# Rewriting the last stage of a recurrent mixture-of-experts layer: other engines, another number of buffers, other order of transfers

## The chip, the cores and the metric

The kernel runs on one core of one Trainium2 chip. The metric is the device time of one execution in microseconds. Five engines matter: TensorE (PE in the profile, its weight loads PEld), VectorE (DVE), ScalarE (ACT), GpSimd (POOL) and SyncE (SP), which here only issues transfers. All of them work on SBUF, the on-chip memory of 128 partitions; DMA engines move data between it and HBM.

## The reference

The input x has 2 x 2048 tokens of 512 channels in float32. Cut to what matters:

```python
xn = layernorm(x)                          # (x - mean) / sqrt(var + 1e-5), each token
# a recurrent layer over the tokens of each sequence
x_conv = silu(conv4(xn) + conv_b)
delta, B_in, C_in = projections(x_conv)
h_t = exp(delta * A) * h_(t-1) + delta * B_in * x_conv     # 16 states per channel
s = sum_n(h * C_in) + xn * D_param
# a mixture of 8 experts, the best 2 of each token, capacity 1024
y = sum_over_2_choices(gate * (gelu(disp @ fc1_w + fc1_b) @ fc2_w + fc2_b))
g = silu(y)
out = x + s * g
```

## The kernel before

Three functions run one after the other, each in a block of its own with its own semaphores and memory; all engines meet between two of them. `front` computes mean and rstd of every token, the routing, and the inputs of the recurrence. `main_loop` runs the experts on TensorE beside the recurrence on VectorE; it leaves `sum_n(h * C_in)` in HBM as `s_rows` and the experts' weighted sum y as `moe_rows`. `tail` is the last stage and the only function that differs between the two kernels: `out = x + (xn * D + s) * silu(y)`.

`tail` goes over the 4096 tokens in NP = 16 pieces of 256 tokens. A piece is a tile of 128 partitions x 2 x 512 values, 512 KB. Each piece has three loads (x into `t_x`, `s_rows` into `t_s`, `moe_rows` into `t_y`) and one store (`t_o`). There are RING = 4 buffers of each kind. For a piece p with its buffer u = p mod 4 the steps are:

- `normalise` (L1177, VectorE): two instructions of 128x512, `o = (x - mean) * rstd`. It waits for all three loads (`in{u}`) and for the store that last used the buffer (`out{u}`).
- `skip` (L1162, GpSimd): `o = o * D`, one instruction of 128x1024, when `xn` says that normalise is done.
- `silu` (L1152, ScalarE): `g = silu(y)`, into a buffer of its own.
- `combine` (L1182, L1185, L1187, VectorE): `o = o + s`, `o = o * g`, `o = o + x`, each one instruction of 128x1024, each waiting for the one before through a semaphore. The first also waits for `skip`.

VectorE runs normalise of piece p+1 ahead of combine of piece p. The order of the transfers is that of SyncE's program: the loads of the first four pieces, and then, for each piece, its store (L1133, when `sum` says that the piece is done) and the three loads (L1126 to L1128) of the piece four later. Each engine's program is a loop of four rounds of four pieces (VectorE's last round is written out).

Of the kernel before, what the change touches and what calls it, by code (L numbers as in the profile page):

```python
# [29 lines left out]
ALU = mybir.AluOpType  # L30
ACT = mybir.ActivationFunctionType
AX = mybir.AxisListType.X
ds = bass.ds

P = 128
B, T, D = 2, 2048, 512
# [11 lines left out]
NT = S // P  # L48
# [30 lines left out]
def memory(nc, ctx):  # L79
    def sb(name, shape, dt=F32):  # L80
        return ctx.enter_context(nc.sbuf_tensor(name, shape, dt))

    def psum(name, shape):
        return ctx.enter_context(nc.psum_tensor(name, shape, F32))

    def sems(prefix, names):
        return {n: ctx.enter_context(nc.semaphore(prefix + n)) for n in names.split()}

    return sb, psum, sems
# [1005 lines left out]
def tail(nc, a, dr, keep, out):  # L1095

    with ExitStack() as ctx:
        sb, psum, sems = memory(nc, ctx)
        TPP = 2
        RING = 4  # L1100
        PC, NP = TPP * P, NT // TPP
        d_row = sb("t_D", [P, D])
        s = sb("t_s", [P, RING, TPP, D])
        y, x = sb("t_y", [P, RING, TPP, D]), sb("t_x", [P, RING, TPP, D])
        g, o = sb("t_g", [P, RING, TPP, D]), sb("t_o", [P, RING, TPP, D])
        rings = " ".join(f"in{u} out{u}" for u in range(RING))
        s_ = sems("t_", f"consts {rings} silu xn skip whole gated sum")
        block = ctx.enter_context(nc.Block())

        def over_rings(eng, body):  # L1110

            with eng.Fori(0, NP // RING) as i:
                for u in range(RING):
                    body(RING * i + u, i, u)

        @block.sync
        def _(sp):
            for u in range(RING):
                sp.sem_inc(s_[f"out{u}"], 16)  # L1119
            sp.dma_start(d_row[:], a["D"].to_broadcast([P, D])).then_inc(s_["consts"], 16)  # L1120

            def load(c, half, p, u):


                sp.wait_ge(s_["sum"], p + 1)
                sp.dma_start(x[:, u], a["x"][ds(c, 1), :, TPP * half:TPP * (half + 1), :].rearrange("o p j d -> p (o j) d")).then_inc(s_[f"in{u}"], 16)  # L1126
                sp.dma_start(s[:, u], dr.s[ds(p * PC, PC)].rearrange("(j p) d -> p j d", p=P)).then_inc(s_[f"in{u}"], 16)  # L1127
                sp.dma_start(y[:, u], dr.y[ds(p * PC, PC)].rearrange("(j p) d -> p j d", p=P)).then_inc(s_[f"in{u}"], 16)  # L1128

            def store(p, u):  # L1130

                sp.wait_ge(s_["sum"], p + RING + 1)
                sp.dma_start(out[ds(p, 1)].rearrange("o (j p) d -> p (o j) d", p=P), o[:, u]).then_inc(s_[f"out{u}"], 16)  # L1133

            for u in range(RING):
                load(u // 2, u % 2, u, u)
            with sp.Fori(1, NP // RING) as i:
                for u in range(RING):
                    store(RING * i + u - RING, u)
                    load(RING // 2 * i + u // 2, u % 2, RING * i + u, u)  # L1140
            for u in range(RING):
                store(NP - RING + u, u)
            for u in range(RING):
                sp.wait_ge(s_[f"out{u}"], 16 * NP // RING + 16)

        @block.scalar
        def _(act):
            def silu(p, i, u):
                act.wait_ge(s_[f"in{u}"], 48 * i + 48)

                act.wait_ge(s_["gated"], p + 1)
                act.activation(g[:, u], y[:, u], ACT.Silu).then_inc(s_["silu"], 1)  # L1152

            over_rings(act, silu)

        @block.gpsimd
        def _(pool):
            pool.wait_ge(s_["consts"], 16)

            def skip(p, i, u):  # L1160
                pool.wait_ge(s_["xn"], p + 1)
                pool.tensor_tensor(o[:, u], o[:, u], d_row[:].unsqueeze(1).to_broadcast([P, TPP, D]), ALU.mult).then_inc(s_["skip"], 1)  # L1162

            over_rings(pool, skip)

        @block.vector
        def _(dve):
            for name in ("whole", "gated", "sum"):
                dve.sem_inc(s_[name], RING)

            def normalise(p, i, u):
                dve.wait_ge(s_[f"in{u}"], 48 * i + 48)

                dve.wait_ge(s_[f"out{u}"], 16 * i + 16)  # L1174
                for j in range(TPP):
                    mean, rstd = (keep[k][:].rearrange("p c j -> p (c j)")[:, ds(TPP * p + j, 1)] for k in ("mean", "rstd"))
                    op = dve.tensor_scalar(o[:, u, j, :], x[:, u, j, :], mean, rstd, ALU.subtract, ALU.mult)  # L1177
                op.then_inc(s_["xn"], 1)

            def combine(p, u):  # L1180
                dve.wait_ge(s_["skip"], p + 1)
                dve.tensor_tensor(o[:, u], o[:, u], s[:, u], ALU.add).then_inc(s_["whole"], 1)  # L1182
                dve.wait_ge(s_["whole"], p + RING + 1)  # L1183
                dve.wait_ge(s_["silu"], p + 1)  # L1184
                dve.tensor_tensor(o[:, u], o[:, u], g[:, u], ALU.mult).then_inc(s_["gated"], 1)  # L1185
                dve.wait_ge(s_["gated"], p + RING + 1)
                dve.tensor_tensor(o[:, u], o[:, u], x[:, u], ALU.add).then_inc(s_["sum"], 1)  # L1187


            normalise(0, 0, 0)  # L1190
            with dve.Fori(0, NP // RING - 1) as i:  # L1191
                for u in range(RING):
                    normalise(RING * i + u + 1, i + (u + 1) // RING, (u + 1) % RING)
                    combine(RING * i + u, u)
            for u in range(RING):
                if u < RING - 1:
                    normalise(NP - RING + u + 1, NP // RING - 1, u + 1)
                combine(NP - RING + u, u)


def build(nc, a, out):
    dr = Scratch(nc)
    with ExitStack() as ctx:
        sb, _, _ = memory(nc, ctx)
        keep = {
            "mean": sb("mean_keep", [P, NCH, TPC]),
            "rstd": sb("rstd_keep", [P, NCH, TPC]),
            "b1": sb("b1_keep", [P, E * HID // P]),
            "neg_a": sb("neg_a_keep", [P, N, KT]),
            "row": sb("row_keep", [P, E + 1, TILES], I32),  # L1210
            "add_row": sb("add_row_keep", [P, E + 1, TILES], I32),
            "gate": sb("gate_keep", [P, E, TILES]),
            "ct": sb("ct_keep", [P, NT, N]),
            "going": sb("going_keep", [P, NCH + 1]),
        }
        front(nc, a, dr, keep)
        main_loop(nc, a, dr, keep)
        tail(nc, a, dr, keep, out)
# [63 lines left out]
```

## Time and profile before

| what | value |
|---|---|
| median of 3 runs | 2216.96 us (2212.52 to 2220.56) |
| the profiled execution, time | 2222.13 us |
| the profiled execution, span from first to last instruction | 2220.3 us |
| last stage in it: first load issued / end of the span | 2101.4 us / 2220.3 us |

Times in the rows are microseconds from the start of the span. "Busy" is time in which an engine worked on an instruction. The share of the whole span (VectorE 88%, TensorE 85%) is an average over all three stages; the last stage is the stretch from 2101 us on, in which TensorE does nothing.

### The profile page before, as it was taken

To read this page: it belongs to the slowest core of one execution; us is meant where nothing else is said; L and a number is where in the kernel's file an instruction comes from. 1 tells how busy PE (TensorE), PEld (TensorE's weight loads), DVE (VectorE), ACT (ScalarE), POOL (GpSimd) and SP (SyncE) were. 2 spreads that over 40 slices of the span, in tenths; PEclk is the share of its full clock that TensorE was granted. 3 is DMA by queue.
4 is the path that set the end of the run, shared out by engine and by line. 5 is a ranking of instruction groups with operands and counts; after the bars stand their busy time and mean duration, and the time that the engine had idled before them with its cause. 6 is when DMAs were issued, how large, how long until landed. Compare 5 with 4: busy or idle time off the path is not lost. (4 is left out here: it accounts for less than half of the span.)

```text
span 2220.3 us, 30939 instructions
## 1 busy us (share of the span) xinstructions
PE 1890.7 (85%) x9160; PEld 1483.9 (67%) x9160; DVE 1955.3 (88%) x2102; ACT 1177.1 (53%) x1714; POOL 1383.9 (62%) x606
## 2 busy tenths in 40 slices
PE   6666729999999999999999999999999999999500
PEld 3222327788788778877887788777877787788400
DVE  6788848989998999899989998998899889998699
ACT  3365635466556555565555556555655565556121
POOL 1267657566756775667566756675667566756454
PEclk9787959999999999999999999999999999999855
DMA  9624354123512441244124412441244124312597
GB/s 292 226 59 93 82 206 95 57 67 128 114 62 67 129 110 62 67 141 102 57 67 144 100 57 71 139 100 57 71 150 89 57 71 144 95 57 81 117 319 250
DMA packets 89192, 246.96 MB, mean 111 GB/s; under 512 B 13296, under 2 KB 14320, under 8 KB 77808
## 3 DMA queue, kind: packets, MB, share of 16 engines
q1 hardware_dynamic: 70640, 207.30, 28.1%
q0 software_dynamic: 18176, 37.83, 9.3%
q8 instruction: 72, 1.18, 0.2%
q10 hardware_dynamic: 256, 0.26, 0.1%
q14 instruction: 48, 0.39, 0.1%
HBM read 173.66 MB, written 71.70 MB: 111 GB/s over the span
## 5 line engine op out<-in xcount | busy, mean ns | idle before, releaser
L976 POOL TENSOR_TENSOR ub_sb<-u_sb,brow_sb 128x1024 f32<-128x1024 f32 x256 | 642.6, 2510 | 463.0 <-DVE a_sb L1071 460.2
L1071 DVE TENSOR_TENSOR_SCAN a_sb<-a_sb,state,ub_sb 128x512 f32<-128x512 f32 x512 | 876.6, 1752 | 12.1 <-issue 7.8
L738 PE MATMUL pm<-xTh,w1l 128*128 128x512 f32 x1024 | 429.4, 419 | 14.9 <-DVE part L1059 6.5
L738 PE MATMUL pm<-w2h,hl 128*128 128x512 f32 x1024 | 423.9, 414 | 0.0
L740 PE MATMUL pm<-xTh,w1h 128*128 128x512 f32 x1024 | 405.9, 396 | 0.0
L739 PE MATMUL pm<-xTl,w1h 128*128 128x512 f32 x1024 | 403.5, 394 | 0.0
L740 PE MATMUL pm<-w2h,hh 128*128 128x512 f32 x1024 | 402.7, 393 | 0.0
L739 PE MATMUL pm<-w2l,hh 128*128 128x512 f32 x1024 | 399.6, 390 | 0.0
L1037 DVE SCALAR_TENSOR_TENSOR s_acc<-pt,ct_keep,s_acc 128x512 f32<-128x512 f32 x480 | 353.1, 736 | 28.3 <-PE pt L768 27.4
L768 PE MATMUL pt<-m_ident,a_sb 128*128 128x128 f32 x2048 | 311.2, 275 | 54.0 <-DVE a_sb L1071 46.3
L768 PEld LDWEIGHTS pt<-m_ident,a_sb 128*128 128x128 f32 x2048 | 251.7, 140 | 131.1 <-issue 55.6
L879 ACT ACTIVATE a_sb<-delta_sb,neg_a_keep 128x512 f32<-128x512 f32 x512 | 330.1, 713 | 6.5
L902 ACT ACTIVATE hh<-pm,b_keep 128x512 fp32r<-128x512 f32 x256 | 176.3, 689 | 219.0 <-PE pm L740 214.9
L1046 DVE TENSOR_TENSOR hl<-pm,hh 128x512 fp32r<-128x512 f32 x256 | 174.6, 682 | 70.7 <-ACT pm L903 66.0
L738 PEld LDWEIGHTS pm<-xTh,w1l 128*128 128x128 f32 x1024 | 196.4, 192 | 50.2 <-DVE part L1059 8.6
L740 PEld LDWEIGHTS pm<-xTh,w1h 128*128 128x128 f32 x1024 | 195.3, 191 | 45.1
L740 PEld LDWEIGHTS pm<-w2h,hh 128*128 128x128 f32 x1024 | 192.6, 188 | 43.5
L872 ACT ACTIVATE state<-a_sb,going_keep 128x4 f32 (+1 forms) x96 | 28.6, 298 | 362.3 <-PE pt L768 362.3
L739 PEld LDWEIGHTS pm<-xTl,w1h 128*128 128x128 f32 x1024 | 196.8, 192 | 33.5
L739 PEld LDWEIGHTS pm<-w2l,hh 128*128 128x128 f32 x1024 | 194.0, 189 | 32.8
L1059 DVE SCALAR_TENSOR_TENSOR part<-pm,gate_keep,part 128x512 f32<-128x512 f32 x256 | 188.5, 736 | 30.7 <-PE pm L740 28.3
L738 PEld LDWEIGHTS pm<-w2h,hl 128*128 128x128 f32 x1024 | 193.4, 189 | 30.9
(130 smaller groups left out, 2286.0 us busy)
## 6 DMA issues: line engine op xcount, KB each, us to landing
w_raw<-in_w SPq DMA_DIRECT2D x64, 1024.0 KB, 5.0
brow_sb<-b_chunks SPq DMA_DIRECT2D x128, 256.0 KB, 3.7
moe_rows<-zeros_sb SPq DMA_DIRECT2D x5, 2048.0 KB, 17.2
xin_sb<-in_x SPq DMA_DIRECT2D x8, 1024.0 KB, 6.2
xn_rows<-xn_sb SPq DMA_DIRECT2D x8, 1024.0 KB, 8.5
delta_chunks<-ln_sb SPq DMA_DIRECT2D x8, 1024.0 KB
u_chunks<-u_now_sb SPq DMA_DIRECT2D x16, 512.0 KB
delta_sb<-delta_chunks SPq DMA_DIRECT2D x8, 1024.0 KB, 8.6
```

The costliest lines, as they stand in the source:

```text
L738: pe.matmul(out, sl, mh, start=start, stop=False)
L739: pe.matmul(out, sh, ml, start=False, stop=False)
L740: return pe.matmul(out, sh, mh, start=False, stop=stop)
L768: mm = pe.transpose(pt[:, bank(s, last), kt * P:(kt + 1) * P], abuf[:, m, kt, tb * P:(tb + 1) * P], ident[:])
L872: act.activation(state[:, ds(q * NPQ * KT + (m - NPQ) * KT, KT)].unsqueeze(2), ends, ACT.Copy, scale=going(e + 1)).then_inc(s_["carried"], 1)
L879: op = act.activation(abuf[:, m, kt, :], delta[:, kt, :], ACT.Exp, scale=keep["neg_a"][:].rearrange("p n k -> p (n k)")[:, ds(col, 1)])
L902: act.activation(hh[:, g, j, :], pm[:, j, :], ACT.Gelu, bias=bias)
L976: pool.tensor_tensor(ub[:, h], u[:, 2 * h:2 * h + 2, :], brow[:, m % 2:m % 2 + 1, :].to_broadcast([P, 2, CH]), ALU.mult).then_inc(s_["bmul ...
L1037: dve.scalar_tensor_tensor(out=acc, in0=h, scalar=c, in1=acc, op0=ALU.mult, op1=ALU.add).then_inc(s_["summed"], 1)
L1046: dve.tensor_tensor(hl[:, g, j, :], pm[:, j, :], hh[:, g, j, :].bitcast(F32), ALU.subtract).then_inc(s_["h_free"], 1)
L1059: dve.scalar_tensor_tensor(out=part[:, t, :], in0=pm[:, t % 4, :], scalar=gate, in1=part[:, t, :], op0=ALU.mult, op1=ALU.add).then_inc(s_[ ...
L1071: op = dve.tensor_tensor_scan(abuf[:, m, 2 * h + k, :], abuf[:, m, 2 * h + k, :], ub[:, h, k, :], state[:, ds(col, 1)], ALU.mult, ALU.add)
```

## The change

`tail` is written anew. ScalarE normalises: two `activation` instructions of 128x512 per piece with the function Identity, `o = rstd * x + shift`, where `shift = -mean * rstd` is computed once for all tokens by one VectorE instruction. ScalarE also takes silu, now in place in `t_y`. VectorE does four instructions of 128x1024 per piece: `* D`, `+ s`, `* silu(y)`, `+ x`. GpSimd has no instruction left in the stage. There are 12 buffers instead of 4 and no `t_g`, the code is unrolled, and the loads of 12 pieces are issued before the first store. Each piece has its own semaphores, one for x and s together, one for y, one for the store.

```diff
-        RING = 4
+        RING = 12
...
-            for u in range(RING):
-                load(u // 2, u % 2, u, u)
-            with sp.Fori(1, NP // RING) as i:
-                for u in range(RING):
-                    store(RING * i + u - RING, u)
-                    load(RING // 2 * i + u // 2, u % 2, RING * i + u, u)
+            for p in range(RING):
+                load(p)
+            for p in range(NP):
+                store(p)
+                if p + RING < NP:
+                    load(p + RING)
...
-            def skip(p, i, u):
-                pool.wait_ge(s_["xn"], p + 1)
-                pool.tensor_tensor(o[:, u], o[:, u], d_row[:].unsqueeze(1).to_broadcast([P, TPP, D]), ALU.mult).then_inc(s_["skip"], 1)
...
+            act.wait_ge(s_["shift"], 1)
+
+            def normalise(p):
+                u = p % RING
+                act.wait_ge(s_[f"xs{p}"], 32)
+                if p >= RING:
+                    act.wait_ge(s_[f"out{p - RING}"], 16)
+                for j in range(TPP):
+                    t = TPP * p + j
+                    op = act.activation(o[:, u, j, :], x[:, u, j, :], ACT.Identity, bias=shift[:, t:t + 1],
+                                        scale=keep["rstd"][:].rearrange("p c j -> p (c j)")[:, t:t + 1])
+                op.then_inc(s_["xn"], 1)
+
+            def silu(p):
+                u = p % RING
+                act.wait_ge(s_[f"y{p}"], 16)
+                act.activation(y[:, u], y[:, u], ACT.Silu).then_inc(s_["silu"], 1)
+
+            for p in range(NP):
+                normalise(p)
+                silu(p)
...
+            dve.scalar_tensor_tensor(out=shift[:], in0=mean, scalar=-1.0, in1=rstd, op0=ALU.mult, op1=ALU.mult).then_inc(s_["shift"], 1)
+            dve.wait_ge(s_["consts"], 16)
+            for p in range(NP):
+                u = p % RING
+                dve.wait_ge(s_["xn"], p + 1)
+                dve.tensor_tensor(o[:, u], o[:, u], d_row[:].unsqueeze(1).to_broadcast([P, TPP, D]), ALU.mult).then_inc(s_["skip"], 1)
                 dve.wait_ge(s_["skip"], p + 1)
                 dve.tensor_tensor(o[:, u], o[:, u], s[:, u], ALU.add).then_inc(s_["whole"], 1)
...
-                dve.tensor_tensor(o[:, u], o[:, u], g[:, u], ALU.mult).then_inc(s_["gated"], 1)
...
+                dve.tensor_tensor(o[:, u], o[:, u], y[:, u], ALU.mult).then_inc(s_["gated"], 1)
```

On VectorE this is what stands in its program for one piece before, in the middle of the loop (normalise of the next piece, then combine of this one; ISA and REGISTER_ALU rows are waits and addresses):

```order
L1177 ISA [waits t_out2,t_in2]
L1177 TENSOR_SCALAR t_o<-t_x,mean_keep,rstd_keep 128x512
L1177 ISA
L1177 TENSOR_SCALAR t_o<-t_x,mean_keep,rstd_keep 128x512
L1182 TENSOR_TENSOR t_o<-t_o,t_s 128x1024 [waits t_skip]
L1183 REGISTER_ALU
L1185 TENSOR_TENSOR t_o<-t_o,t_g 128x1024 [waits t_silu,t_whole]
L1187 TENSOR_TENSOR t_o<-t_o,t_x 128x1024 [waits t_gated]
```

and this at the start of VectorE's part of the stage now; the last four rows come sixteen times:

```order
L1159 SCALAR_TENSOR_TENSOR t_shift<-mean_keep,rstd_keep 128x32
L1164 TENSOR_TENSOR t_o<-t_o,t_D 128x1024 [waits t_xn,t_consts]
L1166 TENSOR_TENSOR t_o<-t_o,t_s 128x1024 [waits t_skip]
L1169 TENSOR_TENSOR t_o<-t_o,t_y 128x1024 [waits t_silu,t_whole]
L1171 TENSOR_TENSOR t_o<-t_o,t_x 128x1024 [waits t_gated]
```

The two normalising instructions and all waits for transfers have left VectorE; a multiply by `t_D` has come, and no wait for GpSimd is left.

On ScalarE the beginning of the stage is now this, the first piece and the normalising of the second (`t_xs0` and `t_y0` are the landings of the first piece's x and s, and of its y):

```order
L1143 ACTIVATE t_o<-t_x,t_shift,rstd_keep 128x512 [waits t_xs0,t_shift]
L1143 ACTIVATE t_o<-t_x,t_shift,rstd_keep 128x512
L1150 ACT_TABLE_LOAD
L1150 ACTIVATE t_y<-t_y 128x1024 [waits t_y0]
L1143 ACTIVATE t_o<-t_x,t_shift,rstd_keep 128x512 [waits t_xs1]
```

One ACT_TABLE_LOAD stands in the whole stage, where the loop before had one in each of its four rounds.

On SyncE, the queue of the transfers, this follows the 36 loads of the first twelve pieces; four such groups of a store and three loads come, and then the last stores without a load between them:

```order
L1121 DMA out<-t_o 128x2x512 [waits t_sum]
L1115 DMA t_x<-in_x 128x1024
L1116 DMA t_s<-s_rows 128x2x512
L1117 DMA t_y<-moe_rows 128x2x512
L1121 DMA out<-t_o 128x2x512 [waits t_sum] x12
```

Before, twelve loads stood ahead of the first store, and twelve such groups followed.

## Rows read from the trace of the kernel before

**Rows 1.** Chain that ended last, from 2085 us on, by line:

```profile
by line: DVE t_o L1185 36.9%; DVE t_o L1182 13.5%; issue 11.1%; DVE t_o L1177 10.7%; DMA t_y<-moe_rows 7.0%; DVE t_o L1187 1.4%; DVEq L1177 1.4%; SPq L1126 0.8%; SPq L1127 0.7%; DVEq L1183 0.4%; SPq L1128 0.3%; SPq L1120 0.3%; DVEq L1174 0.
```

**Rows 2.** Timeline of one round: start, duration, engine, line, operation [idle before]:

```profile
2147.11 1.00 DVE L1177 TENSOR_SCALAR t_o<-t_x,mean_keep,rstd_keep 128x512 f32<-128x512 f32 x2
...
2148.02 1.22 DVE L1182 TENSOR_TENSOR t_o<-t_o,t_s 128x1024 f32<-128x1024 f32 x1
2148.18 3.26 POOL L1162 TENSOR_TENSOR t_o<-t_o,t_D 128x1024 f32<-128x1024 f32 x1 [3.34 <-DVE t_o L1177]
...
2149.27 3.25 DVE L1185 TENSOR_TENSOR t_o<-t_o,t_g 128x1024 f32<-128x1024 f32 x1
...
2152.55 1.22 DVE L1187 TENSOR_TENSOR t_o<-t_o,t_x 128x1024 f32<-128x1024 f32 x1
2153.70 1.00 DVE L1177 TENSOR_SCALAR t_o<-t_x,mean_keep,rstd_keep 128x512 f32<-128x512 f32 x2
```

**Rows 3.** The last piece on VectorE, same columns:

```profile
2213.02 1.22 DVE L1182 TENSOR_TENSOR t_o<-t_o,t_s 128x1024 f32<-128x1024 f32 x1
2214.27 1.23 DVE L1185 TENSOR_TENSOR t_o<-t_o,t_g 128x1024 f32<-128x1024 f32 x1
2215.53 1.23 DVE L1187 TENSOR_TENSOR t_o<-t_o,t_x 128x1024 f32<-128x1024 f32 x1
```

**Rows 4.** The first pieces on ScalarE, VectorE and GpSimd, same columns:

```profile
2109.23 1.00 DVE L1177 TENSOR_SCALAR t_o<-t_x,mean_keep,rstd_keep 128x512 f32<-128x512 f32 x2 [20.56 <-DMA t_y<-moe_rows]
2109.30 1.28 ACT L1152 ACT_TABLE_LOAD   x1 [23.98 <-DMA t_y<-moe_rows]
2110.32 2.34 POOL L1162 TENSOR_TENSOR t_o<-t_o,t_D 128x1024 f32<-128x1024 f32 x1 [21.03 <-DVE t_o L1177]
...
2113.93 1.06 ACT L1152 ACTIVATE t_g<-t_y 128x1024 f32<-128x1024 f32 x1 [2.27 <-DMA t_y<-moe_rows]
...
2117.76 1.06 ACT L1152 ACTIVATE t_g<-t_y 128x1024 f32<-128x1024 f32 x1 [2.77 <-DMA t_y<-moe_rows]
...
2121.51 1.06 ACT L1152 ACTIVATE t_g<-t_y 128x1024 f32<-128x1024 f32 x1 [2.70 <-DMA t_y<-moe_rows]
```

**Rows 5.** Windows: length, busy us (count) of each engine, clock, DMA share, GB/s:

```profile
core 0: us, PE busy (x) PEld busy (x) DVE busy (x) ACT busy (x) POOL busy (x), PEclk, DMA share, GB/s
2112.00:2120.00 8.00, 0.00 (x0) 0.00 (x0) 5.79 (x5) 2.11 (x2) 3.92 (x2) 0.50 1.01 399
2134.00:2199.95 65.95, 0.00 (x0) 0.00 (x0) 65.27 (x51) 13.13 (x12) 32.57 (x10) 0.50 0.96 320
2214.00:2216.00 2.00, 0.00 (x0) 0.00 (x0) 1.93 (x3) 0.00 (x0) 0.00 (x0) 0.50 0.68 262
```

**Rows 6.** DMA issues of the stage: all packets, and s of the first piece:

```profile
DMA packets 15506, 33.84 MB, mean 282 GB/s; under 512 B 1040, under 2 KB 1040, under 8 KB 15504
...
L1127 SPq DMA_DIRECT2D t_s<-s_rows x1: 427/427/427, 2101.9 to 2101.9; - x1
DMA to landing us min/median/max: 6.0/6.0/6.0
```

**Rows 7.** ScalarE's groups by form over the whole span: count, busy us, mean ns:

```profile
L879 ACT ACTIVATE a_sb<-delta_sb,neg_a_keep 128x512 f32<-128x512 f32 x512 | 330.1, 713 | 6.5
...
L377 ACT ACTIVATE z_sb<-pT,chan_sb 128x512 f32<-128x512 f32 x32 | 20.1, 679 | 33.9 <-DVE back_sb L587 33.7
...
L354 ACT ACTIVATE xnT_sb<-conv_sb 128x512 f32 x28 | 15.6, 616 | 8.8 <-DVE conv_sb L506 8.8
```

**Rows 8.** Transfers that SyncE's queue issued, start, duration of the issue:

```profile
2106.47 0.47 SPq L1126 DMA_DIRECT2D t_x<-in_x  x1
2106.99 1.98 SPq L1127 DMA_DIRECT2D t_s<-s_rows  x1
2109.02 1.96 SPq L1128 DMA_DIRECT2D t_y<-moe_rows  x1
```

More of the change, by code:

```diff
@@ L1099, in tail @@
         TPP = 2
-        RING = 4
+        RING = 12
         PC, NP = TPP * P, NT // TPP
[L1102 to L1107, printed above, removed]
+        d_row, shift = sb("t_D", [P, D]), sb("t_shift", [P, NT])
@@ L1108, in tail @@
+        s, y, x, o = (sb(f"t_{n}", [P, RING, TPP, D]) for n in "syxo")
+        parts = " ".join(f"xs{p} y{p} out{p}" for p in range(NP))
+        s_ = sems("t_", f"consts {parts} shift silu xn skip whole gated sum")
         block = ctx.enter_context(nc.Block())
-        def over_rings(eng, body):
-            with eng.Fori(0, NP // RING) as i:
-                for u in range(RING):
-                    body(RING * i + u, i, u)
         @block.sync
         def _(sp):
-            for u in range(RING):
-                sp.sem_inc(s_[f"out{u}"], 16)
@@ L1120, in _ @@
             sp.dma_start(d_row[:], a["D"].to_broadcast([P, D])).then_inc(s_["consts"], 16)
-            def load(c, half, p, u):
-                sp.wait_ge(s_["sum"], p + 1)
-                sp.dma_start(x[:, u], a["x"][ds(c, 1), :, TPP * half:TPP * (half + 1), :].rearrange("o p j d -> p (o j) d")).then_inc(s_[f"in{u}"], 16)
-                sp.dma_start(s[:, u], dr.s[ds(p * PC, PC)].rearrange("(j p) d -> p j d", p=P)).then_inc(s_[f"in{u}"], 16)
-                sp.dma_start(y[:, u], dr.y[ds(p * PC, PC)].rearrange("(j p) d -> p j d", p=P)).then_inc(s_[f"in{u}"], 16)
@@ L1130, in store @@
[L1130 to L1135, printed above, removed]
-                load(u // 2, u % 2, u, u)
-            with sp.Fori(1, NP // RING) as i:
-                for u in range(RING):
-                    store(RING * i + u - RING, u)
-                    load(RING // 2 * i + u // 2, u % 2, RING * i + u, u)
-            for u in range(RING):
-                store(NP - RING + u, u)
@@ L1143, in _, with load @@
-            for u in range(RING):
-                sp.wait_ge(s_[f"out{u}"], 16 * NP // RING + 16)
+            def load(p):
+                u, c, half = p % RING, p // 2, p % 2
+                rows = slice(p * PC, (p + 1) * PC)
+                sp.dma_start(x[:, u], a["x"][c, :, TPP * half:TPP * (half + 1), :]).then_inc(s_[f"xs{p}"], 16)
+                sp.dma_start(s[:, u], dr.s[rows].rearrange("(j p) d -> p j d", p=P)).then_inc(s_[f"xs{p}"], 16)
+                sp.dma_start(y[:, u], dr.y[rows].rearrange("(j p) d -> p j d", p=P)).then_inc(s_[f"y{p}"], 16)
@@ L1146, in _, with store @@
+            def store(p):
+                sp.wait_ge(s_["sum"], p + 1)
+                sp.dma_start(out[p].rearrange("(j p) d -> p j d", p=P), o[:, p % RING]).then_inc(s_[f"out{p}"], 16)
+            for p in range(RING):
[5 more added lines that the diff above has]
+            for p in range(NP):
+                sp.wait_ge(s_[f"out{p}"], 16)
         @block.scalar
         def _(act):
[L1148 to L1158, printed above, removed]
-            def skip(p, i, u):
-                pool.wait_ge(s_["xn"], p + 1)
-                pool.tensor_tensor(o[:, u], o[:, u], d_row[:].unsqueeze(1).to_broadcast([P, TPP, D]), ALU.mult).then_inc(s_["skip"], 1)
-            over_rings(pool, skip)
+            act.wait_ge(s_["shift"], 1)
[9 more added lines that the diff above has]
+                op.then_inc(s_["xn"], 1)
@@ L1166, in _ @@
+            def silu(p):
[5 more added lines that the diff above has]
+                silu(p)
         @block.vector
         def _(dve):
[L1168 to L1178, printed above, removed]
@@ L1180, in combine @@
-            def combine(p, u):
+            mean, rstd = (keep[k][:].rearrange("p c j -> p (c j)") for k in ("mean", "rstd"))
+            dve.scalar_tensor_tensor(out=shift[:], in0=mean, scalar=-1.0, in1=rstd, op0=ALU.mult, op1=ALU.mult).then_inc(s_["shift"], 1)
+            dve.wait_ge(s_["consts"], 16)
+            for p in range(NP):
+                u = p % RING
+                dve.wait_ge(s_["xn"], p + 1)
+                dve.tensor_tensor(o[:, u], o[:, u], d_row[:].unsqueeze(1).to_broadcast([P, TPP, D]), ALU.mult).then_inc(s_["skip"], 1)
@@ L1181, in combine @@
                 dve.wait_ge(s_["skip"], p + 1)
                 dve.tensor_tensor(o[:, u], o[:, u], s[:, u], ALU.add).then_inc(s_["whole"], 1)
-                dve.wait_ge(s_["whole"], p + RING + 1)
+                dve.wait_ge(s_["whole"], p + 1)
                 dve.wait_ge(s_["silu"], p + 1)
-                dve.tensor_tensor(o[:, u], o[:, u], g[:, u], ALU.mult).then_inc(s_["gated"], 1)
-                dve.wait_ge(s_["gated"], p + RING + 1)
+                dve.tensor_tensor(o[:, u], o[:, u], y[:, u], ALU.mult).then_inc(s_["gated"], 1)
@@ L1187, in combine @@
+                dve.wait_ge(s_["gated"], p + 1)
                 dve.tensor_tensor(o[:, u], o[:, u], x[:, u], ALU.add).then_inc(s_["sum"], 1)
[L1190 to L1198, printed above, removed]
```

## The prediction, made before the changed kernel ran

> **What bounds the kernel now.** The change is in the last stage alone, so I first asked the chain of waits what that stage hangs on. From 2085 us on, its largest item is one VectorE instruction, the multiply of L1185, with 36.9% [rows 1]; nothing of a transfer stands there but 7.0%, the opening. Then I read the timeline of one piece in the middle [rows 2]. A piece takes 2153.70 - 2147.11 = 6.59 us, and VectorE is never idle in it: normalise 1.00, add 1.22, multiply 3.25, add 1.22, less small overlaps. What stands out is that the multiply takes 3.25 us where the adds of the same shape take 1.22. In the last piece the same L1185 takes 1.23 [rows 3]. The difference is GpSimd: in the middle its multiply runs from 2148.18 to 2151.44, and L1185 ends at 2152.52, 1.08 us after it. In the last piece GpSimd is idle. GpSimd suffers too: 3.26 us in company of the add, 2.34 alone [rows 2, 4]. So the two behave as if they took turns: GpSimd first waits about 1 us for the add, then VectorE waits until GpSimd is through. VectorE bounds the stage, and about 2 of its 6.6 us per piece are waiting.
>
> The Trainium skill's page "SBUF — State Buffer", section "SBUF: two separate sides", says just that: an exclusive lock on a port pair between a GpSimd instruction and a VectorE instruction with two SBUF inputs, in which the loser waits for the whole instruction. By that rule the 2 us go when GpSimd has no work. A view without it, in which L1185 is a slow multiply on its own account, is the last rival below; the 1.23 us of the last piece speak against it.
>
> Last, the transfers. In the steady stretch the DMA engines are busy to 0.96 at 320 GB/s; in the opening, when nothing but loads is queued, they give 399 GB/s at a share of 1.01 [rows 5]. 320 GB/s is simply VectorE's pace (a piece moves 4 x 0.524 = 2.10 MB; 2.10 MB / 6.59 us = 318 GB/s), yet the share of 0.96 says that there is little air left. That is the danger of this change.
>
> **The change, part by part.**
>
> *VectorE.* Per piece it drops two normalising instructions (1.00) and about 2.03 us of waiting, and takes on one multiply by D. I have no row of that multiply on VectorE. Bounds: below, the 1.22 us of an add of the same shape and operands; above, 3.25, what the other multiply takes now. I take 1.23, since L1185 without GpSimd took that [rows 3]. Each instruction waits for the one before through a semaphore: the starts in the last piece are 2213.02, 2214.27, 2215.53, so 1.255 us from one to the next. A piece is 4 x 1.255 = 5.02 us, sixteen are 80.3 us.
>
> *ScalarE.* Per piece it gets two instructions of 128x512 with scale and bias. The nearest rows are 616, 679 (a bias from SBUF) and 713 ns (a scale from SBUF) [rows 7]: between 1.23 and 1.43, I take 1.4. With silu's 1.06 that makes about 2.5 us a piece, half of VectorE's 5.02: covered, from the second piece on. If the cover were gone it would cost at most 2.5 us once per piece; it would take a table load of 1.28 twice per piece, and the program shows one in all.
>
> *The start.* Before, everything waited for y of the first piece, which was there at 2109.2 [rows 4]. Now x and s are enough for normalise; s was issued at 2101.9 and landed 6.0 later, at 2107.9 [rows 6]. Normalise to 2107.9 + 0.1 + 1.4 = 2109.4, and VectorE starts there. Silu of the first piece: table load at 2109.4, silu from 2110.7 to 2111.8; VectorE wants it after two instructions, at 2111.9, so it is just hidden. The one small VectorE instruction for `shift` runs during the loads' landing and costs nothing; if the landing did not cover it, it would be well under 1.2 us, once.
>
> *The end.* VectorE ends at 2109.4 + 80.3 = 2189.7. From the end of the last add now (2215.53 + 1.23 = 2216.76) to the end of the span (2220.3) there are 3.5 us for the last store. 2189.7 + 3.5 = 2193.2.
>
> *Do the transfers keep up?* Silu's waits show y of pieces 1, 2 and 3 landing before 2113.93, 2117.76 and 2121.51 [rows 4]: 3.8 us for the three loads of a piece, against VectorE's 5.02. From 2121.5, eight more pieces: the loads of twelve pieces are in at 2121.5 + 8 x 3.8 = 2151.9. SyncE does not run far ahead of that: after some ten transfers each issue takes 2 us where it took 0.5 [rows 8], so the first store, though its piece is done at 2114.4, goes out only near 2140 (ten transfers, some 12 us, before 2151.9) and lands about 2155. Who waits for it? ScalarE's normalise of piece 12, which VectorE wants at 2109.4 + 12 x 5.02 = 2169.6: 13 us to spare. Behind it come four groups of a store and three loads. At 399 GB/s a group takes 5.3 us, at the mixed rate of the middle 320 / 0.96 = 333 GB/s it takes 6.3: y of piece 15 is in between 2173 and 2177, ScalarE is done with it 2.5 us later, and VectorE wants it at 2184.7. Meanwhile finished pieces pile up: eleven stores (4 to 14) at 262 / 0.68 = 385 GB/s [rows 5] or 1.36 us each make 15 us, so the queue is empty between 2188 and 2192, when the last store arrives at 2189.7. That adds between 0 and 3 us; I take 0.
>
> *Unrolled code, more semaphores, more buffers.* Nothing but waits on landed transfers; I cost them at nothing because each engine's program now runs ahead of a transfer or of VectorE. If the first instructions came late, it would be paid once, 1 to 2 us.
>
> *Sum* against the profiled execution's own span: 2220.3 - 2193.2 = 27.1 us less, so 2222.13 becomes 2195. The profiled execution lies 5.2 us above the median of 2216.96; on the median the forecast is 2190 (-1.2%). By pieces: 16 x (6.59 - 5.02) = 25.1, and some 2 from the earlier start.
>
> **The rivals.**
>
> *A. The transfers become the bound.* The share of 0.96 speaks for it, the 399 GB/s of the opening against it. If the whole stage only gets 333 GB/s, 33.84 MB [rows 6] take 101.6 us from about 2102.5; the end is at 2204 + 1, 15 us less than now: 2202. The Trainium skill would put it between: "DMA: Bandwidth & Descriptors", section "Where 436 GB/s comes from", lets HBM bind at about 358 GB/s per core. An estimate from this page is 94.5 us of transfers and a time near 2194. The trace does not agree with 358 as a limit here, since it held 399 over 8 us; its chance is part of A's.
>
> *B. The gain is eaten elsewhere and nothing is to be measured.* Loads slower than the opening make ScalarE wait for the first store, which lies behind 36 loads. With 6.2 us for the loads of a piece, twelve take 74 and four groups of 6.2 + 1.4 another 30; with the last piece's work (2.5 + 5.0) and the store (3.5) that is 2102.5 + 115 = 2218. It needs loads at 254 GB/s, and none of the windows with loads alone shows that. Time 2214.
>
> *C. Slower.* L1185's 3.25 us are not GpSimd's doing but belong to a multiply beside transfers, and the new multiply by D takes as long. Then a piece is 2 x 1.255 + 2 x 3.27 = 9.05 us, the stage 144.8, the end 2257.7: time 2254. It decides against the change as soon as the four instructions average (2216.8 - 2109.4) / 64 = 1.68 us. For it: fifteen of sixteen L1185 are long. Against it: the last is not, and each long one ends 1.1 us after GpSimd.
>
> **How the numbers follow.** Runs of one kernel here lie within 0.2% of their median (2212.52 to 2220.56), so 0.3%, 6.7 us, is about what can be told from no change. The forecast has 0.83, A 0.10, B 0.04, C 0.03. The forecast's own range: DMA backlog 0 to +3, start 0 to +2, VectorE at 1.22 instead of 1.255 -2, the spread of the runs ±4: 2184 to 2199. For 8 in 10 over all cases I stretch it to A: 2183 to 2202. Faster by over 0.3% are the forecast and A and no others, 0.93; same 0.04; slower 0.03.
>
> **What would show it.** In the profile of the changed kernel: L1164, L1166, L1169 and L1171 all between 1.20 and 1.25 us and back to back, 5.0 us a piece (wrong if any is over 1.5: C); VectorE's first multiply near 2109.4; ScalarE busy half the time and waiting for VectorE nowhere; the idle time of VectorE between pieces, if any, ended by ScalarE, and ScalarE's by a transfer (A) or by `out0` (B); the first store issued near 2140; the last landing 2.7 to 6 us after its issue. The prediction is wrong if VectorE is idle for more than a few us after the second piece.

## The result, and the profile after

| | before | after |
|---|---|---|
| median of 6 runs | 2215.31 us (2211.73 to 2223.63) | 2185.38 us (2179.89 to 2192.14) |
| profiled execution, span | 2220.3 us | 2186.5 us |
| ratio of times, 95% interval | | 0.9856 [0.9833, 0.9879] |

The change takes 29.9 us, 1.35%, off the median; the ratio on record is not the quotient of the two medians, 0.9865, which lies inside its interval. The forecast was 2190 us. The last stage, from the issue of the load of D to the end of the span, was 119.3 us in the profiled execution before (2101.04 to 2220.3) and is 90.65 us now (2095.85 to 2186.5). That is 28.6 us; the rest of the 33.8 us between the two spans lies ahead of the stage, in code that is the same (experiment 9 shows that it comes and goes from run to run).

The groups of instructions of the last stage in the changed kernel (line, engine, operation, count, busy us, mean ns, idle time before and what ended it):

```profile
L1143 ACT ACTIVATE t_o<-t_x,t_shift,rstd_keep 128x512 f32<-128x512 f32 x32 | 24.3, 806 | 48.5 <-DMA t_s<-s_rows 48.5
L1171 DVE TENSOR_TENSOR t_o<-t_o,t_x 128x1024 f32<-128x1024 f32 x16 | 19.6, 1225 | 0.5
L1169 DVE TENSOR_TENSOR t_o<-t_o,t_y 128x1024 f32<-128x1024 f32 x16 | 19.6, 1225 | 0.6
L1166 DVE TENSOR_TENSOR t_o<-t_o,t_s 128x1024 f32<-128x1024 f32 x16 | 19.6, 1225 | 0.5
L1164 DVE TENSOR_TENSOR t_o<-t_o,t_D 128x1024 f32<-128x1024 f32 x16 | 19.5, 1218 | 8.3 <-ACT t_o L1143 8.3
L1150 ACT ACTIVATE t_y<-t_y 128x1024 f32<-128x1024 f32 x16 | 16.7, 1042 | 0.0
```

All four VectorE instructions take 1.22 us, the multiply by silu(y) too, and the multiply by D that no row of before had priced takes the same. VectorE waited once: 8.3 us before its first multiply. One piece in the middle, and the opening and the end, from the timeline (start, duration, engine, line):

```profile
2095.85 0.35 SPq L1110 DMA_DIRECT2D t_D<-in_D  x1
...
2102.72 1.52 ACT L1143 ACTIVATE t_o<-t_x,t_shift,rstd_keep 128x512 f32<-128x512 f32 x2 [22.09 <-DMA t_s<-s_rows]
...
2104.34 1.23 DVE L1164 TENSOR_TENSOR t_o<-t_o,t_D 128x1024 f32<-128x1024 f32 x1 [8.25 <-ACT t_o L1143]
...
2123.09 1.52 ACT L1143 ACTIVATE t_o<-t_x,t_shift,rstd_keep 128x512 f32<-128x512 f32 x2 [1.52 <-DMA t_s<-s_rows]
...
2124.00 1.22 DVE L1164 TENSOR_TENSOR t_o<-t_o,t_D 128x1024 f32<-128x1024 f32 x1
...
2125.25 1.22 DVE L1166 TENSOR_TENSOR t_o<-t_o,t_s 128x1024 f32<-128x1024 f32 x1
...
2126.51 1.23 DVE L1169 TENSOR_TENSOR t_o<-t_o,t_y 128x1024 f32<-128x1024 f32 x1
...
2127.77 1.23 DVE L1171 TENSOR_TENSOR t_o<-t_o,t_x 128x1024 f32<-128x1024 f32 x1
...
2128.91 1.22 DVE L1164 TENSOR_TENSOR t_o<-t_o,t_D 128x1024 f32<-128x1024 f32 x1
...
2137.37 1.72 SPq L1121 DMA_DIRECT2D out<-t_o  x1
...
2147.02 1.52 ACT L1143 ACTIVATE t_o<-t_x,t_shift,rstd_keep 128x512 f32<-128x512 f32 x2 [1.51 <-DMA t_s<-s_rows]
...
2152.15 1.52 ACT L1143 ACTIVATE t_o<-t_x,t_shift,rstd_keep 128x512 f32<-128x512 f32 x2 [2.66 <-DMA t_s<-s_rows]
...
2181.82 1.23 DVE L1171 TENSOR_TENSOR t_o<-t_o,t_x 128x1024 f32<-128x1024 f32 x1
```

A piece is 2128.91 - 2124.00 = 4.91 us where it was 6.59 [rows 2]. Within a piece the starts are 1.25 us apart; from the last instruction of a piece to the first of the next it is only 1.14. ScalarE's two normalising instructions wait for the landing of s each time, never for the store: the first store, issued at 2137.37, landed 12.2 us later, at 2149.6, and the inputs of piece 12, which takes its buffer, only at 2152.1. The windows over the loads alone and over nearly the full stage (length, busy of PE, PEld, DVE, ACT, POOL, clock, DMA share, GB/s), which answers to [rows 5]:

```profile
2108.00:2136.00 28.00, 0.00 (x0) 0.00 (x0) 27.42 (x24) 17.34 (x22) 0.00 (x0) 0.50 1.04 395
```

```profile
2108.00:2180.00 72.00, 0.00 (x0) 0.00 (x0) 70.49 (x60) 36.12 (x44) 0.00 (x0) 0.50 1.05 400
```

VectorE is busy 98%, and the transfers run at 400 GB/s over a window with loads alone up to 2137 and stores from there on, where they ran at 320 before.

### The profile page after: what moved, and what is told of

Same layout as the page of the kernel before. It is cut to its first block and busy times, and to the rows that moved or that the text cites. A ratio compares the mean times of both kernels' runs of the same rounds, so it can differ in the third digit from the quotient of the medians.

```text
span 2186.5 us, 30720 instructions
## 1 busy us (share of the span) xinstructions
PE 1892.6 (87%) x9160; PEld 1483.1 (68%) x9160; DVE 1935.5 (89%) x2087; ACT 1196.1 (55%) x1743; POOL 1334.3 (61%) x590
## 5 line engine op out<-in xcount | busy, mean ns | idle before, releaser
L1071 DVE TENSOR_TENSOR_SCAN a_sb<-a_sb,state,ub_sb 128x512 f32<-128x512 f32 x512 | 883.8, 1765 | 10.3 <-issue 7.7
L738 PE MATMUL pm<-xTh,w1l 128*128 128x512 f32 x1024 | 429.2, 419 | 14.4 <-DVE part L1059 10.8
L872 ACT ACTIVATE state<-a_sb,going_keep 128x4 f32 (+1 forms) x96 | 28.6, 298 | 361.1 <-PE pt L768 361.1
```

The source lines that it names most:

```text
L738: pe.matmul(out, sl, mh, start=start, stop=False)
L872: act.activation(state[:, ds(q * NPQ * KT + (m - NPQ) * KT, KT)].unsqueeze(2), ends, ACT.Copy, scale=going(e + 1)).then_inc(s_["carried"], 1)
L1071: op = dve.tensor_tensor_scan(abuf[:, m, 2 * h + k, :], abuf[:, m, 2 * h + k, :], ub[:, h, k, :], state[:, ds(col, 1)], ALU.mult, ALU.add)
```

## The experiments

Medians and ratios are against runs of the kernel before on the same chip. Since the stages ahead of the last vary by several us (they end between 2086.6 and 2101.0 us in the profiles here), the last column, the length of the last stage in the profiled execution (issue of the load of D to end of span), tells more than the time. Experiments 1 to 4 ran together, with a median before of 2217.55 us; 5 to 8 together, with 2215.62 us.

| run | median us | ratio [95%] | last stage us |
|---|---|---|---|
| 1 before, GpSimd's multiply on VectorE | 2201.46 | 0.9927 [0.9903, 0.9952] | 2091.14 to 2200.1: 109.0 |
| 2 after, multiply by D on GpSimd | 2198.41 | 0.9925 [0.9901, 0.9949] | 2090.53 to 2194.2: 103.7 |
| 3 after, 4 buffers | 2187.27 | 0.9870 [0.9832, 0.9907] | 2091.24 to 2182.2: 91.0 |
| 4 after, last add left out | 2185.72 | 0.9876 [0.9822, 0.9930] | 2095.27 to 2184.1: 88.8 |
| 5 after again | 2189.40 | 0.9875 [0.9850, 0.9899] | 2097.47 to 2187.8: 90.3 |
| 6 after, first piece loaded early | 2182.97 | 0.9860 [0.9837, 0.9883] | 2094.72 to 2181.2: 86.5 |
| 7 after, 3 buffers | 2196.37 (1 run) | | 2100.49 to 2194.8: 94.3 |
| 8 after, 2 buffers | 2222.05 (1 run) | | 2097.51 to 2220.5: 123.0 |
| 9 before again | 2207.81 (1 run; another on the same chip: 2209.00) | | 2086.56 to 2206.0: 119.4 |

**Experiment 1: the kernel before, with GpSimd's work on VectorE.** GpSimd's block is gone.

```diff
...
-            def skip(p, i, u):
-                pool.wait_ge(s_["xn"], p + 1)
-                pool.tensor_tensor(o[:, u], o[:, u], d_row[:].unsqueeze(1).to_broadcast([P, TPP, D]), ALU.mult).then_inc(s_["skip"], 1)
...
             def combine(p, u):
+                dve.wait_ge(s_["xn"], p + 1)
+                dve.tensor_tensor(o[:, u], o[:, u], d_row[:].unsqueeze(1).to_broadcast([P, TPP, D]), ALU.mult).then_inc(s_["skip"], 1)
                 dve.wait_ge(s_["skip"], p + 1)
...
```

> The kernel before with one edit: the multiply by D runs on VectorE, ahead of the add of s, and GpSimd has no work in the last stage. Turns theory (GpSimd and VectorE exclude each other): every multiply takes 1.2 us, a piece is 0.91 + 4 x 1.25 + 1.15 - 1.25 = 5.8 us from the gaps of the round in the middle, 16 x 0.78 = 12.5 us less than before, about 2203 us. Rival (a multiply beside transfers is slow by itself): the multiply by g stays at 3.25 us and the one by D takes as long, a piece is near 10 us, over 50 us more.

A round in its middle, timeline, same columns:

```profile
2144.89 1.00 DVE L1167 TENSOR_SCALAR t_o<-t_x,mean_keep,rstd_keep 128x512 f32<-128x512 f32 x2
2145.80 1.22 DVE L1172 TENSOR_TENSOR t_o<-t_o,t_D 128x1024 f32<-128x1024 f32 x1
2147.06 1.23 DVE L1174 TENSOR_TENSOR t_o<-t_o,t_s 128x1024 f32<-128x1024 f32 x1
2148.32 1.22 DVE L1177 TENSOR_TENSOR t_o<-t_o,t_g 128x1024 f32<-128x1024 f32 x1
...
2149.58 1.23 DVE L1179 TENSOR_TENSOR t_o<-t_o,t_x 128x1024 f32<-128x1024 f32 x1
2150.72 1.00 DVE L1167 TENSOR_SCALAR t_o<-t_x,mean_keep,rstd_keep 128x512 f32<-128x512 f32 x2
```

VectorE has one instruction more per piece and a piece is shorter: 5.83 us, as expected. The multiply by g takes 1.22 us beside running transfers. The rival, a slow multiply, falls. The stage gains 10.3 us, not 12.5. My expectation was made from the round in the middle and left out the opening: with the multiply on VectorE, which sits in program order behind normalise of the second piece, it begins only when that piece is in, while GpSimd did it during that wait [rows 4]. So 15 turns of 2.03 us are saved and 16 multiplies of 1.26 us (start to start) are paid: 30.4 - 20.2 = 10.2.

**Experiment 2: the changed kernel, with the multiply by D back on GpSimd.**

```diff
...
+                pool.wait_ge(s_["xn"], p + 1)
+                pool.tensor_tensor(o[:, u], o[:, u], d_row[:].unsqueeze(1).to_broadcast([P, TPP, D]), ALU.mult).then_inc(s_["skip"], 1)
...
-                dve.wait_ge(s_["xn"], p + 1)
-                dve.tensor_tensor(o[:, u], o[:, u], d_row[:].unsqueeze(1).to_broadcast([P, TPP, D]), ALU.mult).then_inc(s_["skip"], 1)
                 dve.wait_ge(s_["skip"], p + 1)
...
```

> The changed kernel with one edit: the multiply by D runs on GpSimd again; ScalarE still normalises, 12 buffers, unrolled. Turns theory: three VectorE instructions of 1.22 us and one of GpSimd of 2.3 us exclude each other, so a piece costs 3.7 + 2.3 = 6.0 us or more, against 4.91: 17 to 20 us more than the changed kernel, about 2204 us. Rival (VectorE was bound by its own number of instructions, and GpSimd's work beside it is free): VectorE needs 3.75 us per piece, the transfers (33.8 MB at 399 GB/s, 85 us) bound, 1 to 3 us less than the changed kernel.

VectorE and GpSimd in this run, timeline:

```profile
2107.30 3.10 POOL L1162 TENSOR_TENSOR t_o<-t_o,t_D 128x1024 f32<-128x1024 f32 x1 [1.32 <-ACT t_o L1143]
2108.24 3.25 DVE L1174 TENSOR_TENSOR t_o<-t_o,t_y 128x1024 f32<-128x1024 f32 x1
...
2147.24 1.23 DVE L1174 TENSOR_TENSOR t_o<-t_o,t_y 128x1024 f32<-128x1024 f32 x1
...
2148.32 2.35 POOL L1162 TENSOR_TENSOR t_o<-t_o,t_D 128x1024 f32<-128x1024 f32 x1 [2.20 <-ACT t_o L1143]
2148.50 3.25 DVE L1176 TENSOR_TENSOR t_o<-t_o,t_x 128x1024 f32<-128x1024 f32 x1
...
2151.67 1.21 DVE L1171 TENSOR_TENSOR t_o<-t_o,t_s 128x1024 f32<-128x1024 f32 x1
```

One VectorE instruction fewer per piece, and the stage is 13.0 us longer than the changed kernel's. Whichever VectorE instruction meets GpSimd's takes 3.24 to 3.37 us: in these rows L1174 once and L1176 once, elsewhere in the run L1171 too, multiply or add. It ends 1.1 us after GpSimd's (2110.40 and 2111.49; 2150.67 and 2151.75), and once GpSimd has done all sixteen, every instruction is back at 1.22. GpSimd is done at 2166.43, ahead of VectorE, since it follows ScalarE and that the landings; VectorE's last six pieces take 3.65 us each. So taking turns is shown, and the rival, that GpSimd's work beside VectorE is free, falls.

The direction was right and the size was not: 13 us, not 17 to 20. I charged each turn with GpSimd's own 2.3 us; what VectorE loses by one is 3.25 - 1.22 = 2.03 us: its instruction begins some 0.2 us after GpSimd's 2.34 us do (2148.50 against 2148.32) and ends 1.1 us after them instead of 1.22. GpSimd's first multiply met nothing, so there are 15 turns in 16 pieces: from 2101.30 (first of VectorE) to 2190.70 (its end) it is 5.59 us per piece, 10.7 us more in all than in the changed kernel. The other 2.3 us lie in the opening, where the first piece waits for GpSimd's 2.34 us: VectorE's first instruction on a piece comes 10.8 us after the first issue instead of 8.5.

**Experiments 3, 7 and 8: 4, 3 and 2 buffers instead of 12.**

```diff
-        RING = 12
+        RING = 4        # 3 in experiment 7, 2 in experiment 8
```

> The changed kernel with 4 buffers instead of 12, so that 12 loads instead of 36 stand ahead of the first store. If the buffers and the loads far ahead do nothing for the time: within 2 us of the changed kernel, since the loads of a piece are issued three pieces, 14.7 us, before they are wanted and landed within 10 us in the kernel before. Rival (the deep queue is what lets loads and stores share 400 GB/s): the rate falls to the 320 to 333 GB/s of the kernel before, a piece takes 6.3 us, about 20 us more than the changed kernel.

> The changed kernel with 3 buffers. The loads of a piece are issued 9.8 us before VectorE wants it; they land 6 to 7 us after the issue and ScalarE takes 1.5. So it still fits: a stage of 91 to 93 us. Rival (anything under four buffers starves VectorE): over 95 us, VectorE idle between pieces, ended by ScalarE and that by the load of s.

> The changed kernel with 2 buffers. A piece is wanted 4.9 us after its loads are issued, they need 0.6 + 6.3 + 1.5 us, so two pieces take 8.3 + 4.9 = 13.2 us, 6.6 each: a stage of about 90.7 + 14 x 1.7 = 115 us, as long as before the change. Rival (the queue answers faster when little is in it, y after s costs nothing): 5.5 us a piece, 100 us.

The windows of 4, 3 and 2 buffers, one row each in this order:

```profile
2120.00:2170.00 50.00, 0.00 (x0) 0.00 (x0) 48.70 (x42) 24.76 (x30) 0.00 (x0) 0.50 1.05 407
```

```profile
2120.00:2170.00 50.00, 0.00 (x0) 0.00 (x0) 47.92 (x40) 23.34 (x29) 0.00 (x0) 0.50 1.04 404
```

```profile
2120.00:2200.00 80.00, 0.00 (x0) 0.00 (x0) 56.63 (x47) 27.72 (x34) 0.00 (x0) 0.50 0.91 293
```

With 4 buffers the stage is 91.0 us, the same as with 12, and the transfers run at 407 GB/s though stores and loads alternate from the start. So the deep queue is not what makes 400 GB/s, and the rival falls. But four buffers are just enough for sixteen pieces. VectorE's pieces are 4.91 us apart until near the end, and ScalarE gets its inputs every 5.14; the lead of the opening is used up with three pieces to go:

```profile
2163.49 1.23 DVE L1164 TENSOR_TENSOR t_o<-t_o,t_D 128x1024 f32<-128x1024 f32 x1
...
2167.07 1.52 ACT L1143 ACTIVATE t_o<-t_x,t_shift,rstd_keep 128x512 f32<-128x512 f32 x2 [2.67 <-DMA t_s<-s_rows]
...
2168.62 1.23 DVE L1164 TENSOR_TENSOR t_o<-t_o,t_D 128x1024 f32<-128x1024 f32 x1
...
2173.76 1.23 DVE L1164 TENSOR_TENSOR t_o<-t_o,t_D 128x1024 f32<-128x1024 f32 x1
```

That costs 0.7 us here (VectorE's sixteen pieces take 79.4 us instead of 78.7). An estimate from these rows: with many more pieces, VectorE would fall back to 5.14 us a piece, 0.23 us more.

With 3 buffers the stage is 94.3 us, a little over what I expected. In the timeline of that run VectorE now waits for ScalarE, and ScalarE for s, by a hair:

```profile
2143.08 1.52 ACT L1143 ACTIVATE t_o<-t_x,t_shift,rstd_keep 128x512 f32<-128x512 f32 x2 [2.68 <-DMA t_s<-s_rows]
...
2144.63 1.23 DVE L1164 TENSOR_TENSOR t_o<-t_o,t_D 128x1024 f32<-128x1024 f32 x1 [0.15 <-ACT t_o L1143]
...
2148.23 1.52 ACT L1143 ACTIVATE t_o<-t_x,t_shift,rstd_keep 128x512 f32<-128x512 f32 x2 [2.69 <-DMA t_s<-s_rows]
```

All those waits but the opening's come to 1.4 us. From the fifth piece on the pieces are 5.15 us apart but for one of 5.60. That is the pace at which ScalarE's inputs come with 4 buffers too, and the transfers run at 404 GB/s and a share of 1.04, so it reads as the pace of the transfers (2.10 MB / 407 GB/s = 5.15), not a latency; that is argued from these rows, not tested. Against 4 buffers, VectorE's stretch is 2.5 us longer (81.9 against 79.4) and its first instruction on a piece comes 0.8 us later. With 2 buffers the stage is 123.0 us, longer than before the change, and 8 us over my 115; the DMA engines have gaps (share 0.91) and give 293 GB/s. My sum had the pieces at 6.6 us; they take 2147.48 - 2140.76 = 6.72 in this stretch and 6.92 on average (2106.25 to 2217.00), and I had charged the surplus to 14 pieces, not 16:

```profile
2140.76 1.23 DVE L1164 TENSOR_TENSOR t_o<-t_o,t_D 128x1024 f32<-128x1024 f32 x1 [1.98 <-ACT t_o L1143]
...
2145.93 1.52 ACT L1143 ACTIVATE t_o<-t_x,t_shift,rstd_keep 128x512 f32<-128x512 f32 x2 [4.26 <-DMA t_s<-s_rows]
...
2147.48 1.23 DVE L1164 TENSOR_TENSOR t_o<-t_o,t_D 128x1024 f32<-128x1024 f32 x1 [1.72 <-ACT t_o L1143]
```

**Experiment 4: the changed kernel without the last add.**

```diff
-                dve.tensor_tensor(o[:, u], o[:, u], y[:, u], ALU.mult).then_inc(s_["gated"], 1)
-                dve.wait_ge(s_["gated"], p + 1)
-                dve.tensor_tensor(o[:, u], o[:, u], x[:, u], ALU.add).then_inc(s_["sum"], 1)
+                dve.tensor_tensor(o[:, u], o[:, u], y[:, u], ALU.mult).then_inc(s_["sum"], 1)
```

> The changed kernel without the last add (+ x is left out, the output is (xn * D + s) * silu(y)); all transfers stay. VectorE then needs 3.67 us per piece. If the transfers stand right behind VectorE as the bound (33.8 MB at 399 GB/s is 85 us of the 90.7 us stage), only 1 to 3 us are gained on the changed kernel. Rival (VectorE alone is the bound, the queue has air): 16 x 1.23 = 20 us are gained.

VectorE has 19.6 us less to do and the stage is 1.8 us shorter (1.5 against experiment 5). Its last instruction, and the chief waits of this run (who waited for whom, us in total, times, longest):

```profile
2170.98 1.22 DVE L1169 TENSOR_TENSOR t_o<-t_o,t_y 128x1024 f32<-128x1024 f32 x1
```

```profile
ACT t_o L1143 <- DMA t_s<-s_rows: 48.1, 16, 21.3
DVE t_o L1164 <- ACT t_o L1143: 16.8, 16, 7.9
```

VectorE now waits for ScalarE ahead of every one of the sixteen pieces, and ScalarE for the transfers. VectorE is through at 2172.2, 11.9 us before the end of the span at 2184.1, where it was 3.5 us before it. The transfers stand right behind VectorE: 33.85 MB at 400 GB/s are an estimated 85 us, to which the latency at the two ends comes, and the changed kernel is 2 us from what this run, which waits for them, takes.

**Experiments 5 and 6: the changed kernel again, and with the first piece loaded early.** The core of the edit in experiment 6, in SyncE's part of `main_loop` behind the last weights; the weight buffer `w_raw` is kept through the last stage, and 8 buffers stand for 12:

```diff
...
+            sp.dma_start(keep["d_row"][:], a["D"].to_broadcast([P, D])).then_inc(s_["first"], 16)
+            sp.wait_ge(s_["w_lo"], 2 * NCH * NQ + 1)
+            sp.wait_ge(s_["w_hi"], 2 * NCH * NQ + 1)
+            first = raw[:].rearrange("p (k j d) -> p k j d", k=2, j=2)
+            sp.dma_start(first[:, 0], a["x"][0, :, 0:2, :]).then_inc(s_["first"], 16)
+            sp.dma_start(first[:, 1], dr.s[0:2 * P].rearrange("(j p) d -> p j d", p=P)).then_inc(s_["first"], 16)
...
```

> The changed kernel once more, as the control of this set. Its last stage, from the issue of the load of D to the end of the span, was 90.65 us in its first profile; I expect 90.7 within 0.5, while the start of the stage may differ by several us, since the stages before it are the same code and gave starts from 2090.5 to 2101.0 us in the profiles so far.

> The changed kernel with 8 buffers, in which D and the first piece's x and s are loaded at the end of the main loop's transfers, into a weight buffer that is free by then, so that the stage opens with the load of the first y. If the rest of the changed kernel's stage is start latency and then VectorE at 4.91 us a piece: the third VectorE instruction, 11.0 us after the first issue in the changed kernel, starts at about 6, the stage is 86 to 87 us, 4 us less than the changed kernel's (2181 us if that measures 2185). Rival (the transfers bound the whole, started early or not): the first 1.3 MB less of 33.8 MB are worth 3.3 us at 399 GB/s, but the final additions into y's rows are slowed by the early loads and give it back: within 1 us of the changed kernel.

The control gives 90.3 us. The opening of experiment 6, from its timeline:

```profile
2094.72 0.38 SPq L1128 DMA_DIRECT2D t_y<-moe_rows  x1
2095.00 1.52 ACT L1155 ACTIVATE t_o<-w_raw,t_shift,rstd_keep 128x512 f32<-128x512 f32 x2 [16.15 <-DVE t_shift L1171]
...
2096.55 1.22 DVE L1175 TENSOR_TENSOR t_o<-t_o,t_D 128x1024 f32<-128x1024 f32 x1 [1.58 <-ACT t_o L1155]
...
2099.91 1.23 DVE L1180 TENSOR_TENSOR t_o<-t_o,t_y 128x1024 f32<-128x1024 f32 x1 [0.87 <-ACT t_y L1162]
```

The stage, counted from its first issue, that of y, is 86.5 us, 3.8 less than the control, in the expected range. VectorE's first multiply comes 1.8 us after that issue instead of 8.2 in the control, and 2.3 us are lost again to waits for the first y and the second piece. Part of the 3.8 is only where the count begins: in the control the first y is issued 1.3 us after D, and from that issue on the gain is 89.0 - 86.5 = 2.5 us. In whole times the two cannot be told apart (0.9860 and 0.9875, their intervals overlap), so this is a gain read from the profile, not from the clock.

**Experiment 9: the kernel before, profiled again.**

> The kernel before, profiled a second time, as a control of the stages: the last stage was 119.3 us from the issue of the load of D to the end of the span. If what differs from run to run lies in the stages ahead of it, the stage is 119.3 within 0.5 again, while its start is anywhere from 2090 to 2101 us; the rival, that the changed code also shortened the stages before it, wants a start near 2101 again.

The stage is 119.4 us again, and it starts at 2086.56 where it started at 2101.04: 14.5 us between two executions of the same code, and below the 2090 us that I had given as the lower end. The starts of the changed kernel and its variants, 2090.5 to 2100.5, lie within that spread, so nothing shows that the changed code shortened the stages ahead. What makes them vary stays open.

## Why the prediction was right

The mechanism and the sum held, within 1.5 us on a stage of 90.7.

- *VectorE's 2 us per piece are waiting for GpSimd.* Shown from both sides by experiments 1 and 2.
- *The multiply by D costs 1.23 us* (bounds 1.22 and 3.25). It takes 1.218.
- *5.02 us per piece.* It is 4.91. I took the 1.255 us between two starts within a piece for all four; the step to the next piece is 1.14 us. The rows showed it: from L1187 to the next L1177 it is 1.15 [rows 2]. Over sixteen pieces the term is 78.7 us (2104.34 to 2183.05) instead of 80.3, and this is the whole difference to the forecast of the stage, 92.2 us (2193.2 - 2101.0).
- *Start at 8.4 us after the first issue, end 3.5 us after the last add.* 8.5 and 3.45. ScalarE's pair takes 1.52 us where I had 1.4 and an upper bound of 1.43 from the rows of other instructions; it was hidden but for the first. My split of the gain, 25.1 us by pieces and 2 by an earlier start, was loose: VectorE's first instruction on a piece came 8.2 us after the first issue before, so it starts no earlier. Its whole stretch went from 107.5 us (2109.23 to 2216.76) to 78.7, in which the 3.91 us of waiting for the second piece are gone as well.
- *The first store near 2140, for a stage that began at 2101.0.* That is 39 us into the stage; it was 41.5 (2137.37 - 2095.85). Nobody waited for it.
- *Transfers: 5.3 to 6.3 us for a store and three loads.* 2152.15 - 2147.02 = 5.13, a little under the quick end; the loads alone took 4.0 us a piece where I had 3.8. Mixed with stores, the transfers of a piece are thus slower than VectorE's 4.91 us, and the lead of the opening covered it. The backlog of stores that I had taken at 0, out of 0 to 3 us, cost 0: the last store landed 3.4 us after its issue. Rival A, transfers at the 333 GB/s that the mixed stretch of before suggested, was wrong: its 320 GB/s was VectorE's pace, and the share of 0.96 beside it was no sign of a full queue's limit. Mixed traffic gives 400 to 407 GB/s. The Trainium skill ("DMA: Bandwidth & Descriptors", section "Where 436 GB/s comes from") gives about 358 GB/s as HBM's limit for a core, half of what a stack gives to two. The trace does not agree with it as a limit for one core that runs alone: 400 GB/s over 72 us.
- *Rival B* wanted loads at 254 GB/s; they came in at 395 GB/s. *Rival C* fell with experiment 1.
- The forecast of the time, 2190, was 4.6 us over the median, which lies near the lower end of the forecast's own range (2184 to 2199). As a gain, 27.1 us were forecast; it is 28.6 in the stage and 29.9 between the medians. What is beyond the stage is the variation of the stages ahead, and that it came out no larger is luck.

The parts of the change are worth, in us of the last stage: GpSimd's multiply to VectorE 10.3 (experiment 1); ScalarE's normalising, y with a semaphore of its own and the unrolled code together 18.0 (from experiment 1 to experiment 3). No run tells these apart from each other, but the two traces say where they lie: 12.1 us between the first multiply by D and the end of the last add (91.5 to 79.4, chiefly the pair of 0.9 us a piece that left VectorE), and 5.7 us ahead of that multiply (13.9 to 8.2 us after the first issue, of which 3.5 was VectorE's wait for the second piece's y). 12 buffers for 4 are worth 0.3 us, which is within what two profiles of the changed kernel differ by.

## What to carry to other kernels

When an instruction of one shape has two durations in one trace, look at what else ran during the long ones. Such waiting is recorded as busy time (VectorE was busy 65.27 of 65.95 us in [rows 5]), so no view of idle time shows it. Work given to GpSimd beside two-input VectorE instructions in SBUF cost VectorE 2.0 us a piece here, more than the 1.2 us of doing it there. Before counting on more buffers, compute the lead they give (buffers less one, times the piece) against landing plus the first consumer, and the pace of the transfers against that of the engine: 4 sufficed for these sixteen pieces, 3 nearly, 2 undid the whole change. And a high DMA share at a rate that equals the compute engine's pace doesn't tell the ceiling; the ceiling shows where the queue alone is waited for.

## What the runs showed of the hardware that I had not expected

Loads and stores alternating in one queue ran at 407 GB/s (experiment 3), no slower than loads alone at 395 to 399. And the DMA share of 0.96 in the kernel before was reached at 320 GB/s, against 1.05 at 400: the engines counted as busy nearly all the time while a quarter more could be moved.
